# Five packs of the second convolution's input made in the midst of the first, on one core

## The reference

```python
def _sage_conv(h, src, dst, Wl, bl, Wr, num_nodes):
    agg = segment_sum(h[src], dst) / max(degree(dst), 1)
    return agg @ Wl.T + bl + h @ Wr.T
h = _sage_conv(x, ...); h = relu(h); h = _sage_conv(h, ...)      # layer 3, then x = layernorm(x + h)
h = _sage_conv(x, ...); h = elu(h);  h = _sage_conv(h, ...)      # layer 4, then x = layernorm(x + h)
```

## Time and profile before

| what | value |
|---|---|
| median of three timed runs | 4345.51 us |
| the profiled execution's own time | 4349.17 us |
| its span, first to last instruction | 4347.4 us |
| PE, PE loads, DVE, ACT, POOL busy | 73%, 54%, 61%, 36%, 57% |
| mean granted TensorE clock | 0.872 of full speed |

### The profile page before, as it was taken

How to read it: one execution, slowest core, us unless ns; L and a number is a source line. 1 busy time by engine, 2 the same in 40 slices (tenths; PEclk the granted TensorE clock), 3 DMA queues, 4 the chain that set the end, 5 groups by cost and what they waited for, 6 DMA issues and landing times.

```text
span 4347.4 us, 61646 instructions
## 1 busy us (share of the span) xinstructions
PE 3180.2 (73%) x18737; PEld 2359.7 (54%) x18737; DVE 2642.2 (61%) x5826; ACT 1575.2 (36%) x3723; POOL 2483.8 (57%) x2580
## 2 busy tenths in 40 slices
PE   0666666666766766667667776396569999999999
PEld 0444444444645445445445554274447777888777
DVE  5999999999776666666666665810003444333333
ACT  1888888887233333333333333200002111011000
POOL 7777777777777777777777777777770000000000
PEclk9999999999777677776777767698789999999999
DMA  7666666666255545444454553263345666666776
GB/s 256 227 231 226 232 227 230 228 232 213 77 148 133 135 131 136 131 131 133 129 137 131 133 135 87 74 237 119 133 161 199 247 246 244 249 251 237 285 273 220
DMA packets 389479, 802.66 MB, mean 185 GB/s; under 512 B 207626, under 2 KB 264814, under 8 KB 363134
## 3 DMA queue, kind: packets, MB, share of 16 engines
q1 hardware_dynamic: 241208, 591.07, 40.4%
q0 software_dynamic: 82320, 90.28, 9.4%
q10 hardware_dynamic: 65718, 118.62, 7.2%
HBM read 581.03 MB, written 218.64 MB: 184 GB/s over the span
## 4 chain that ended last, share of the span: by engine, by line
POOL 48%; PE 25%; issue 18%; DVE 5%; DMA 4%; ACT 0%; DVEq 0%; SPq 0%; POOLq 0%
POOL area L825 27%; PE ps L1251 21%; POOL adj L908 8%; POOL adj L836 8%; DMA area<-relu_table,early 2%; POOL area L880 2%; POOL dst_table L923 1%; DVE second L1808 1%; DVE area L1824 1%; PE ps L1129 1%; POOL out_ring L810 1%; POOL area L810 1%; DVE second L1763 1%; PE ps L977 1%; DVE second L1818 1%
## 5 line engine op out<-in xcount | busy, mean ns | idle before, releaser
L825 POOL DMA_INDIRECT area<-src_table,early x784 | 749.7, 956 | 239.0 <-issue 238.7
L825 POOL DMA_INDIRECT area<-relu_table,early x784 | 739.7, 944 | 238.9 <-issue 230.7
L993 PE MATMUL ps<-ident,area 128*96 128x128 f32 x1568 | 448.4, 383 | 460.1 <-DMA area<-src_table,early 459.1
L993 PEld LDWEIGHTS ps<-ident,area 128*96 128x96 f32 x1568 | 320.6, 241 | 654.9 <-DMA area<-src_table,early 644.1
L1251 PE MATMUL ps<-second,area 128*128 128x288 bf16 x5194 | 652.3, 287 | 0.2 <-DVE second L1928 0.2
L1251 PEld LDWEIGHTS ps<-second,area 128*128 128x128 f16 x5194 | 508.4, 98 | 129.2 <-DVE second L1928 0.5
L1763 DVE SCALAR_TENSOR_TENSOR second<-second,area,ps 128x512 bf16<-128x512 f32 x784 | 537.5, 738 | 0.0
L1005 PE MATMUL ps<-ident,area 96*128 96x96 f32 x2352 | 424.4, 347 | 138.4 <-ACT out_ring L1320 133.1
L1005 PEld LDWEIGHTS ps<-ident,area 96*128 96x128 f32 x2352 | 357.8, 210 | 231.3 <-DVE area L1824 216.0
L1795 DVE TENSOR_TENSOR_SCAN area<-flags,area,ps 96x512 f32<-96x512 int8 x196 | 250.0, 1275 | 358.1 <-ACT dump L1306 356.3
L908 POOL DMA_INDIRECT adj<-out_ring x390 | 385.9, 989 | 127.1 <-issue 125.9
(11 more groups left out here) (335 smaller groups left out, 4971.2 us busy)
## 6 DMA issues: line engine op xcount, KB each, us to landing
area<-adj SPq DMA_DIRECT2D x147, 1632.0 KB
area<-adj SPq DMA_DIRECT2D x54, 1568.0 KB
adj<-early SPq DMA_DIRECT2D x102, 816.0 KB
soft_sums<-out_ring ACTq DMA_DIRECT2D x196, 384.0 KB
second<-key_dram SPq DMA_DIRECT2D x98, 512.0 KB, 4.1
area<-dst_table SPq DMA_DIRECT2D x784, 48.0 KB
sums<-out_ring ACTq DMA_DIRECT2D x196, 192.0 KB
second<-caps_dram SPq DMA_DIRECT2D x98, 192.0 KB, 4.3
```

The source lines that it names most:

```text
L825: pool.indirect_dma_start(out=src_rows[:, s, c, :], out_offset=None, in_=gather_table[p], in_offset=bass.IndirectOffsetOnAxis(ap=src_cols[ ...
L993: nc.tensor.matmul(ps[0:F, s % 2, at], src_rows[:, s, c, :], ident[:, :], start=False, stop=False)
```

## The change

After tile 20 of convolution 0, every engine does a "first portion" of the hand-over: both joint tiles are summed, and packs 0 to 4 (tiles 0 to 19) are linked, turned, projected and split. For each of the tiles 21 to 47, PE then multiplies the row's first 20 blocks with these new parts too (`begin`), while the row lies in its slot. DVE reduces these sums (`reduce_begun`), ACT stores them to HBM (`store_begun`) and loads all 27 back before convolution 1. After tile 48, joint tile 1 is summed again, and packs 5 to 12 are handed over. In convolution 1 the 27 jobs load and multiply 31 blocks instead of 51, and DVE adds the kept sum. Joint rows are renumbered so that joint tile 0 holds those of the first half of the edges. The SP wait for joint tile 1 in the first portion is one of two: if tile 19 is complete with the early writes, a block of zeros is taken at `adj_ready` 1, else the real block at `adj_ready` 50.

```diff
+    BEGUN_ROUNDS = 4
+    JOINT_ROWS = ET // EXT
+    ZEROS_AT = JOBS
+    BEGUN_FROM = SLOTS + 1 + BEGUN_ROUNDS * SLOTS      # 21
+    BEGUN_PACKS = BEGUN_FROM // PACK                   # 5
+    BEGUN_TILES = BEGUN_PACKS * PACK                   # 20
-        CELLS = JOBS * P * KB * P
+        CELLS = (JOBS + 1) * P * KB * P
...
-        def over_first_jobs(step, eng, between):
+        def over_first_jobs(step, begun_step, eng, first_portion):
...
+            rounds_of(step, head, BEGUN_ROUNDS)
+            first_portion()
+            for j in range(BEGUN_FROM, BEGUN_FROM + SLOTS):
+                begun_step(j, j % SLOTS, j // SLOTS)
+            rounds_of(begun_step, BEGUN_FROM + SLOTS, FIRST_ROUNDS - BEGUN_ROUNDS - 1)
+            rounds_of(begun_step, middle, (tail - middle) // SLOTS)
...
-                    for tile in range(EI, JOBS):
+                    for tile in range(EI, JOBS + 1):
                         clear(tile, 0)
                         clear(tile, 1)
...
+            def fill_first_portion():
+                sp.wait_ge(adj_ready, 1)
+                sp.dma_start(joint_slots[:, 0, :, :]..., adj[NT, :, 0:NT * P]).then_inc(joint_landed, 16)
+                batches = nc.values_load(first_portion_at[0:1, 0:1], ..., min_val=1, max_val=BATCHES + 1)
+                block = nc.values_load(first_portion_at[0:1, 1:2], ..., min_val=NT + 1, max_val=ZEROS_AT)
+                sp.wait_ge(adj_ready, batches)
+                sp.dma_start(joint_slots[:, 1, :, :]..., adj[bass.ds(block, 1), :, 0:NT * P]...).then_inc(joint_landed, 16)
+                sp.wait_ge(linked, 1)
+                sp.dma_start(first_links, links_of(slice(0, BEGUN_TILES))).then_inc(links_landed, 16)
+            def fill_last_joint():
+                sp.wait_ge(adj_ready, BATCHES + 1)
+                sp.wait_ge(linked, EXT + BEGUN_TILES)
+                sp.dma_start(last_joint_slot..., adj[NT + 1, :, 0:NT * P]).then_inc(joint_landed, 16)
-            over_first_jobs(fill_first, sp, lambda: fill_joint(0))
+            over_first_jobs(fill_first, fill_first, sp, fill_first_portion)
+            fill_last_joint()
...
+            def begin(j, lane, nth):                                                  # PE
+                pe.wait_ge(slot_landed[lane], nth * 16 + 16)
+                wait(pe, begun_reduced, j - (BEGUN_FROM + 1))
+                for s in range(BEGUN_TILES):
+                    last = nc.tensor.matmul(bank(2 + lane % 2, P, PARTS_F), slots[:, lane, s, :],
+                                            parts_of_y[1][:, s, :, :]..., start=s == 0, stop=s == BEGUN_TILES - 1)
+                last.then_inc(begun, 1)
+            def first_portion():
+                pe.wait_ge(conv["split"], NT)
+                pe.wait_ge(conv["zkept"], NT)
+                pe.wait_ge(joint_landed, 16 * EXT)
+                for i in reversed(range(EXT)):
+                    sum_up_joint(i, joint_slots[:, i, :, :])
+                pe.wait_ge(links_landed, 16)
+                pe.wait_ge(conv["extended"], EXT)
+                hand_over(0, BEGUN_PACKS, first_links)
+                pe.wait_ge(conv["split"], NT + BEGUN_TILES)
+                pe.wait_ge(conv["zkept"], NT + BEGUN_TILES)
+            over_first_jobs(sum_up_first, begin_and_sum_up, pe, first_portion)
+            pe.wait_ge(joint_landed, 16 * (EXT + 1))
+            sum_up_joint(1, last_joint_slot)
+            hand_over(BEGUN_PACKS, PACKS, links)
...
-                    for s in range(NT if joint else KB):                              # PE, sum_up
+                    for s in range(at_block, NT if joint else KB):
                         if follows and s == turn_at:
                             pe.wait_ge(conv["posted"], k + ((to - 1) * NT + 1))
                             turn_into(to, k, side, layer_out[:, side, :])
...
+            chain.do(v.tensor_scalar(first_portion_at[:, :], tile_ready[:, BEGUN_TILES - 1:BEGUN_TILES]..., -1.0, 1.0, ALU.add, ALU.min))
+            chain.do(v.tensor_scalar(first_portion_at[:, 0:1], first_portion_at[:, 0:1], float(BATCHES), 1.0, ALU.mult, ALU.add))
+            chain.do(v.tensor_scalar(first_portion_at[:, 1:2], first_portion_at[:, 1:2], float(NT + 1 - ZEROS_AT), float(ZEROS_AT), ALU.mult, ALU.add))
...
+            def reduce_begun(j, lane, nth):                                           # DVE
+                dve.wait_ge(begun, j - (BEGUN_FROM - 1))
+                wait(dve, begun_stored[b], 32 * nth + 16 * (lane // 2) - 16 * ((BEGUN_FROM + 1 - b) // 2))
+                v.tensor_reduce(begun_out[:, b, :], bank(2 + b, P, PARTS_F)..., axis=X, op=ALU.add).then_inc(begun_reduced, 1)
...
+                    if begun_row:                                                     # DVE, finish, after the reduce
+                        chain.do(v.tensor_tensor(whole[:, b, :], whole[:, b, :], begun_in[:, bass.ds(k, 1), :]..., ALU.add))
                     to = layer_out[:, b, :] if not q % 2 else mixed_in[:, b, :]
                     joining = v.scalar_tensor_tensor(to, whole[:, b, :], rdeg[:, bass.ds(k, 1)], flat(z_sb), ALU.mult, ALU.add)
```

More of the change, by code:

```diff
@@ L113, in build @@
     FIRST_ROUNDS = 7
-    ROWS_DONE = [1 + math.ceil((min((i + 1) * P * CH, SCATTERS) - EARLY) / BATCH) for i in range(EXT)]
-    assert ROWS_DONE[-1] == BATCHES + 1
+    BEGUN_ROUNDS = 4
+    JOINT_ROWS = ET // EXT
+    ZEROS_AT = JOBS
+    assert JOINT_ROWS * EXT == ET and JOINT_ROWS * CH == EARLY
+    BEGUN_FROM = SLOTS + 1 + BEGUN_ROUNDS * SLOTS
+    BEGUN_PACKS = BEGUN_FROM // PACK
+    BEGUN_TILES = BEGUN_PACKS * PACK
+    BEGUN_ROWS = NT - 1 - BEGUN_FROM
+    LATE_ROUNDS = 4
+    assert EXT + BEGUN_FROM == EXT + 1 + SLOTS + LATE_ROUNDS * SLOTS and BEGUN_ROWS == 27
     ctx = ExitStack()
@@ L419, in build @@
         held = sem("held")
+        begun, begun_reduced = sem("begun"), sem("begun_reduced")
+        begun_stored, begun_landed = [sem(f"begun_stored{b}") for b in range(2)], sem("begun_landed")
         last_half_landed = sem("last_half_landed")
@@ L505, in over_groups, with over_jobs @@
             last(NG - 1)
-        def over_jobs(step, eng, chain=None, steps=0, jobs=JOBS, head=EXT + 1 + SLOTS):
-            tail = jobs - SLOTS
+        def over_jobs(step, eng, chain=None, steps=0, begun_step=None, begun_steps=0):
+            head, tail, last = EXT + 1 + SLOTS, JOBS - SLOTS, JOBS - 1
+            begun_step, begun_steps = begun_step or step, begun_steps or steps
             for j in range(head):
                 step(j, j % SLOTS, j // SLOTS)
[L513 to L516, removed]
-                if chain:
[L518 to L525, removed]
-        def over_first_jobs(step, eng, between):
+            middle = head + LATE_ROUNDS * SLOTS
+            assert (tail - middle) % SLOTS == 0
+            for at, rounds, do, n in ((head, LATE_ROUNDS, step, steps), (middle, (tail - middle) // SLOTS, begun_step, begun_steps)):
+                start = chain.base + chain.n if chain else 0
+                with eng.Fori(0, rounds) as u:
+                    if chain:
+                        chain.base, chain.n = u * (SLOTS * n) + start, 0
+                    for i in range(at, at + SLOTS):
+                        do(u * SLOTS + i, i % SLOTS, u + i // SLOTS)
+                    assert not chain or chain.n == SLOTS * n, chain.n
+                if chain:
+                    chain.base, chain.n = start + rounds * SLOTS * n, 0
+            for j in range(tail, last):
+                begun_step(j, j % SLOTS, j // SLOTS)
+            step(last, last % SLOTS, last // SLOTS)
+        def over_first_jobs(step, begun_step, eng, first_portion):
             head, tail = SLOTS + 1, NT - SLOTS
@@ L1604, in _ @@
             chain.do(v.tensor_scalar(now, now, -1.0, None, ALU.add))
-            v.tensor_copy(first_rank[:, :], now).then_inc(ranks_made, 1)
+            v.tensor_copy(first_rank[:, :], now).then_inc(setup_made, 1)
             for g in range(NG):
@@ L2035, in finish @@
                             dve.wait_ge(out_landed[b], nth * 32 - (16 if b == lane else 0))
+                    if q == 1 and isinstance(k, int) and k == SLOTS:
+                        dve.wait_ge(begun_landed, 16)
+                    if begun_row:
+                        chain.do(v.tensor_tensor(whole[:, b, :], whole[:, b, :],
+                                                 begun_in[:, bass.ds(k, 1), :].rearrange("p a f -> p (a f)"), ALU.add))
                     to = layer_out[:, b, :] if not q % 2 else mixed_in[:, b, :]
@@ L2063, in finish, with finish_begun @@
                         split_into(q + 1, k, b)
-                over_jobs(finish, dve, chain, {1: 4 + 4, 2: 4, 3: 4}[q])
+                def finish_begun(j, lane, nth):
+                    finish(j, lane, nth, q == 1)
+                over_jobs(finish, dve, chain, {1: 4 + 4, 2: 4, 3: 4}[q], finish_begun, {1: 1 + 4 + 4, 2: 4, 3: 4}[q])
 def kernel(**inputs):
```

257 lines of the change are left out of this document (154 added, 103 removed).

## The result

After: 4619.70 us, median of 4 runs (4618.12 to 4621.22). Before, on the same chip: 4345.57 us, median of 4 (4343.73 to 4348.79). The ratio is 1.0629, with a 95% interval of 1.0615 to 1.0642: 274 us slower. The forecast was 4638 us, 18 us too much, inside its range of 4596 to 4664.

The account below looks back on a forecast made before the run. The prediction took POOL's scatters to bound convolution 0 and PE to set the pace elsewhere. 252.7 + 39 + 1 = 292.7 us on the profiled 4349.2 gave 4641.9; less 3.7 us to the median, 4638 us, range 4596 to 4664.

Parts of the forecast that it names:

- Part 1: Convolution 0 and hand-over: SP's new wait for the last scatter batch moves work after tile 20 behind it, costing 252.7 us.
- joint tile 1's load goes out: On SP in convolution 0: count 50 is reached at 3274.2 us, 0 to 3 us earlier as bound.
- first link: On PE, after two joint tiles at 11.96 us plus 1.87 for a slow start, and DVE's 1.8 us extension: 3297 us.
- tile 21's 20 blocks: On PE, after the first portion's five packs, which take 23.0 us: start at 3320.0 us.
- second hand-over: After tile 48, joint tile 1 again and its extension: starts at 3563.1 us, its eight packs taking 26.3 us.
- Part 2: Convolution 1: its 27 shorter jobs take 8.23 us each instead of 6.78, 39 us more; bounds 7 and 58.
- 9/11 of about 1.5, 1.2 us: Clock term per shorter job of convolution 1: idle PE restarts at 1.2 GHz, 1.2 us more; bounds 0 and 1.9.
- 7.03 us a job: Loop over DVE and PE in convolution 1's shorter jobs: one more add of 0.35 us, 0.25 over the earlier mean.
- Rival 1: Convolution 1: the clock holds, so the loop takes 7.03 us a job; 4606 us in all, chance 0.30.
- Rival 2: Convolution 0: the wait lets go at count 1 with zeros, first portion filling PE's idle stretches; 4340 us, chance 0.03.
- Rival 3: Convolution 1: PE's pace saves 66 us, but the wait is for the last batch; 4533 us, chance 0.04.
- Part 3: The rest: three small DVE instructions and two more clears at the start, 1 us for both.

Follow-up runs that it names:

- experiments 1 to 3: experiment 1, Experiment 3 and, between them, the change with three packs made early instead of five, so its wait takes count 1: 4352.39 us, ratio 1.0009.
- experiment 5: Experiment 3 plus 14 unread matmuls ahead of each turn in the 27 shorter jobs of convolution 1: 4341.31 us, ratio 0.9987.
- experiment 6: Experiment 3 with the kept sums scaled and added to `z` for all 27 tiles at once, the add in each job dropped: 4336.02 us, ratio 0.9972.
- experiment 9: experiment 7 with turn and projection at blocks 33 and 38 instead of 28 and 33 in the shorter jobs: 4313.34 us, ratio 0.9918.
- experiment 7: experiment 6 with `x` added to `z` ahead too and the projection 5 blocks behind the turn instead of 10: 4323.12 us, ratio 0.9946.
- Experiment 3: The change with all five packs, joint tile 0 keeping 128 joint rows awaited at count 16, joint tile 1 first taken as zeros: 4357.87 us, ratio 1.0018.
- Experiment 4: Experiment 3 without the begun sums, each job of convolution 1 loading and multiplying all 51 blocks again: 4333.50 us, ratio 0.9964.
- experiment 1: The kernel before with only the change's wait for the joint rows, at its count of 50, added: 4517.07 us, ratio 1.0384.

## Why the prediction was right

**Part 1, 252.7 us forecast, 249.3 measured.** The mechanism is the one forecast, and experiments 1 to 3 show it: the wait alone costs 168 us, and with a count that the rows can meet, part 1 goes altogether. By its steps:

| step | forecast | measured | why they differ |
|---|---|---|---|
| joint tile 1's load goes out | 3274.2 | 3271.5 | POOL's last scatter starts 1.9 us earlier and its signal follows sooner; I had kept 0 to 3 us as bound |
| PE starts | 3281.3 | 3278.0 | 6.5 us to land, not 7.05 |
| first link | 3297 | 3294.7 | 98 matmuls took 14.72 us, not 13.8: the clock stayed at 0.50 for longer, to about 3283 |
| tile 21's 20 blocks | 3320.0 | 3316.3 | five packs 21.6 us, not 23.0 |
| tiles 21 to 47, one | 8.42 + 1.87 once | 8.45, and 2.2 once | as the dense rows had it |
| second hand-over | 3563.1 | 3560.8 | 1.92 us of idle PE; the trace names the links' load, but DVE's extension ended only 0.1 us before |
| convolution 1 | 3589.4 | 3586.0 | 25.2 us, not 26.3 |

The first step is off by 2.7 us and each later one by at most 1.4, so 2.7 of the 3.4 us at the end were there from the start.

**Part 2, 39 us forecast, 22.0 measured.** The direction and both causes, the loop and the clock, were right; the size was off. The mis-sized term is the clock, "9/11 of about 1.5, 1.2 us": it measured 16.3 us over 27 jobs, 0.6 each. The share was wrong: 12 of 27 jobs, not 9 of 11. The price was near, 16.3 / 12 = 1.36 us for a slow job, but partly by luck: it was worked out for ten matmuls at 1.2 GHz between turn and projection, and only five of the 12 slow jobs ran like that. In five others the clock fell behind the projection, and the loop closed over PE's last blocks, which the prediction doesn't have; that this costs about as much is luck. I took the share from gaps in convolution 0, 2.0 to 2.9 us each, and carried it over to gaps of 1.9 to 3.1 us. By the table the slow jobs come and go, at much the same gap lengths and in the same loop, and another kernel with the same code in it has them elsewhere. A share taken from eleven cases was a draw, and its bounds (0 to 1.9 us a job) were the honest part. What sets which jobs are slow stays open.

"7.03 us a job" for the loop of DVE and PE measured 7.06 with the clock held (experiment 5), 7.3 us over the 27 jobs where I had 27 x 0.25 = 7. Here too, errors cancel. The 6.68 us of the earlier trace rows are not the loop's own length: the turn starts 0.32 us behind the end of the norm (3569.80 to 3570.12) with no idle time on PE, so PE was still at its blocks; where PE waits for the norm, this is 0.13 us (3806.35 to 3806.48 above). With 31 blocks and without the add, jobs at full clock take 6.47 to 6.62 us (experiment 6) where before has 6.68 to 6.73. So PE set the pace of before, by 0.1 to 0.2 us a job. Against that, the add takes 0.4 us instead of 0.35, and the first job of every four grows by more than the others, from 7.1 to 7.6 us.

Of the 21.0 us between the forecast for the profiled execution, 4641.9, and its measured 4620.9, 16.1 are this term (27 x 1.2 - 16.3) and 3.4 are part 1's.

**Rival 1, the clock holds (4606 us).** It did not: the windows at 0.50 stand in the trace, and experiment 5 gains 13 to 15 us by nothing but unread matmuls. But the result lies between the two cases, 4606 and 4638, as 12 slow jobs of 27 lie between none and 22. The Trainium skill, "TensorE: Matmul & The Clock Gate" (section "HAM oscillation"), would have had every job at full clock; the trace shows 1.2 GHz behind a gap of 2.74 us, so the measurement decides against it here. In experiment 9 gaps of up to 1.7 us did not do this; in experiment 7 the clock was at 0.50 two us after one of 1.73 us.

**Rival 2, the wait lets go at once (4340 us).** The condition was false, as forecast. Experiment 3 makes it true in another way and came out at 4357.87, not at 4340: the hand-over gave 10.0 us, near the forecast 12.7, but that sum had left the clock out of convolution 1, the very term that I had put into the forecast. With it (7.3 + 12.8 us instead of 7) the rival's sum is 4340 + 2.7 + 13.1 = 4356; the kernel before was 3.3 us slower on that chip than in the sum.

**Rival 3, PE's pace sets convolution 1 (4533 us).** Experiment 4 shows it wrong most plainly: with all 51 blocks back, the jobs are 0.75 us shorter than with 31. Only when the loop itself was cut (6, 7, 9) did the 540 matmuls taken out become time, 27 x (6.79 - 5.75) = 28 us of the 66.

**Part 3** (1 us): the span is 271.8 us longer, 249.3 and 22.0 of which lie in the two parts; 0.5 is left for everything else.

Not tried: a shorter loop with all 51 blocks in convolution 1, where by the prediction's 6.65 us of PE's own work there is little to gain; and reading joint tile 1's rows while POOL still scatters others of its tile, which would let the change's own split of the joint rows start earlier. That is a race.

## What to carry to other kernels

Before moving work into an engine's idle time, look up what its first wait is for, and at which count that is reached in the trace: everything queued behind it in order moves with it. Before taking work out of an engine that shows 100% busy, follow one job round its loop over all engines. And look where nothing waits: a step that starts late without idle time on its engine is that engine's delay and not the loop's. Here the loop was only 0.1 to 0.2 us a job shorter than PE's work, so taking out 40% of PE's work could gain no more than that, and the added add took more, until the loop was cut too.

## What the runs showed of the hardware

- An idle PE can cost more than a busy one: 14 unread matmuls a job made the kernel 13 to 15 us faster, by 27 jobs at a granted clock of 1.00 instead of 0.92. Gaps of 0.8 to 1.7 us ahead of the turns left it at 1.00 in experiment 9; in experiment 7 one of 26 gaps of 1.3 to 1.7 us was followed by 0.50, in the changed kernel 12 of 27 gaps of 1.9 to 3.1 us.
- The clock can fall well after PE has begun again: in five slow jobs of the changed kernel the ten matmuls behind the gap took 1.42 to 1.57 us, near those at full clock (1.39), and the 21 behind the projection 3.96 to 4.11 us instead of 2.74.
- POOL's scatters hardly feel the loads beside them: 0.969 us each in before and after, and from first to last 508.3 and 509.1 us without the loads (after, experiment 1) against 511.9 and 512.3 with them (before, experiment 3).
- The first job in every four is longer than the next ones at full clock: by 0.4 us in before (7.11 against 6.69), 0.6 to 0.7 in experiment 5, 0.2 in 7. The loop over jobs goes round every four, so its turn is the likely cause; it was not tested.
